# Moving five weight subtractions of GpSimd from the last attention heads to the rear of an expert

## The chip, the cores and the metric

One core of a Trainium2 chip runs the whole program in one launch. The metric is the device time of that launch in microseconds. The engines are named as in the profile: PE is TensorE, DVE is VectorE, ACT is ScalarE, POOL is GpSimd and SP is SyncE, which here issues only DMAs.

## What is computed

Input `x` has 1250 rows of 512 numbers; there are 20000 edges. Two blocks follow each other, each added to its input:

```
x = x + gnn(layernorm(x), edges)      # mean over neighbours, two matmuls, batch norm, relu
x = x + moe(layernorm(x))             # 4 experts, every row goes to its best 2

expert(xf, mask):
    h    = ln(xf);   q, k, v = split(h @ in_proj.T + b)          # 8 heads of 64
    a    = softmax(where(mask, q @ k.T / 8, -1e9));  o = (a @ v) @ out_proj.T + b
    x1   = xf + o
    return x1 + gelu(ln(x1) @ w1.T + b1) @ w2.T + b2              # hidden width 256
```

The change lies in the second block. All weights are used there as a sum of two f16 numbers: a high half, and a low half that is the f32 weight minus the high half.

## The kernel before, in words

The four experts run one after the other. A router gives each expert a list of rows; the program holds several bodies ("arms") for different list lengths and every engine branches to the same one. In this run the experts with numbers 0, 1 and 3 take a short arm of 4 row tiles (512 rows), and expert 2 takes the long arm of 10 row tiles (1280 rows). Here they are called the first, second, third and fourth expert.

The weights of an expert are ten pieces of 128 x 1024 numbers: six for the projections to q, k and v (`QKV_P`), two for the output projection, one for each of the two MLP matrices. A piece comes by DMA into one of five slots of `w_stage` (`load_piece`, L482), ACT writes the high half (`high_weights`, L856), and POOL writes the low half as the f32 piece minus the high half (`low_weights`, L587, one TENSOR_TENSOR at L590) and counts `s_elo`. Piece p + 5 may be loaded once the low half of piece p stands (L490), so the next expert's piece 5 waits for its piece 0, and its pieces 6 to 9 wait for its pieces 1 to 4. PE waits for the six projection pieces at L1639, in front of the first value product of the expert.

An expert has two parts. In the first, the heads, PE makes projections, scores and weighted sums, ACT the exponentials, DVE maxima of the scores and, for each pair of heads, the division by the sum of the exponentials (`divide_of`, L2258: a reciprocal L2265, a product L2266, and the two halves of the result L2267 and L2268; it needs ACT's copy of the sums, L1100). With ACT's last heads (`short_head`, L1109, heads 5 to 7; in the long arm spread over the last two heads) come the high halves of the next expert's six projection pieces, and POOL's six low halves stand in its own order behind its work for the heads.

In the second part, the rear, the work runs over pairs of row tiles. PE first runs 18 or 32 matmuls that nobody reads (L1702), then the output projection (`project_out`, L1704). DVE adds the rows (L2365) and takes their statistics (L2369 to L2377); POOL raises the variances to the power -1/2 (L829), one instruction for a pair of tiles; DVE normalises (`second_rows`, L2385); PE transposes (L1724); ACT applies the affine map (L968); DVE splits it into f16 halves (`split_columns`, L2109 and L2110); PE multiplies (L1423), ACT applies gelu (L1188), DVE splits again (L2398, L2399) and adds the expert's share to the running total (`part`, L2391; `give`, L2405). POOL fetches the running totals with indirect DMAs at the start of the rear (L817) and sends the finished rows away at its end (L835), each when `s_y` says that its tile is done.

All five engines run their own instruction lists in the written order; semaphores join them. POOL's list around the change is: the heads' copies, the six low halves of the next expert, the wait for the end of DVE's divisions (L811), the fetches with the powers between them, and the outgoing rows.

Of the kernel before, what the change touches and what calls it, by code (L numbers as in the profile page):

```python
# [29 lines left out]
NE = 4  # L30
# [18 lines left out]
QKV_P, OUT_P, W1_P = (W_OUT - W_QKV) // WP, W_1 // WP, W_2 // WP  # L49
# [111 lines left out]
def program(nc, x, src, dst, gnn_w, gnn_par, gate_w, gate_b, ew, epar_d, erow, out):  # L161
    stack = ExitStack()
    with stack:
# [422 lines left out]
        def _(pool):  # L586
            def low_weights(e, p):  # L587
                cols = slice(p * WP, (p + 1) * WP)
                pool.wait_ge(s_ehi, e * NWP + (p + 1))
                nc.gpsimd.tensor_tensor(w16[:, 1, cols], w_stage[:, p % WB, :], w16[:, 0, cols],  # L590
                                        ALU.subtract).then_inc(s_elo, 1)
# [128 lines left out]
            def expert_pool(e, shape):  # L720
# [14 lines left out]
                def copy_values(j, hd):  # L735
                    nc.gpsimd.tensor_copy(v_head[:, hd, 0:nt, hd * HD:(hd + 1) * HD],  # L736
                                          v_rows[:, 0:nt, bass.ds(j * P + hd * HD, HD)]).then_inc(s_vh, 1)

                def after_head():

                    summed.skip(nx)
                    pool.wait_ge(s_pv, summed.at(0))
                    pool.sem_inc(s_idle, 1)

                def values_of(j, hd):

                    t0 = j % 2 * nt
                    nc.gpsimd.tensor_copy(v_head[:, hd, t0:t0 + nt, hd * HD:(hd + 1) * HD],
                                          v_rows[:, 0:nt, j * P + hd * HD:j * P + (hd + 1) * HD]).then_inc(s_vh, 1)

                def second_head(j):

                    pool.wait_ge(s_split, splits.at(2 * j + 2))
                    pool.sem_inc(s_idle, 1)
                    if j in (0, 3):
                        pool.wait_ge(s_vh, e * H + (2, 0, 0, 8)[j])
                    else:
                        pool.wait_ge(s_elo, e * NWP + QKV_P + (0, 1, 3, 0)[j])
                    pool.sem_inc(s_idle, 1)
                    cols = slice(j % 2 * SHORT, j % 2 * SHORT + nt * P)  # L760
                    nc.gpsimd.tensor_copy(q_both[0:HD, 1, cols], halves[HD:P, 0, 0, cols])
                    nc.gpsimd.tensor_copy(k_both[0:HD, 1, cols], halves[HD:P, 1, 1, cols])
                    nc.gpsimd.tensor_copy(q_both[HD:P, 1, cols], halves[HD:P, 0, 1, cols])
                    nc.gpsimd.tensor_copy(k_both[HD:P, 1, cols], halves[HD:P, 1, 0, cols]).then_inc(s_qkc, 1)
                    pool.wait_ge(s_qkc, seconds.at(j + 1))
                    pool.sem_inc(s_idle, 1)

                if shape.short:
                    values_of(0, 0)
                    values_of(0, 1)  # L770
                    pool.wait_ge(s_scat, 16 * 2 * NT)
                    second_head(0)
                    values_of(1, 0)
                    values_of(1, 1)
                    low_weights(e, QKV_P)
                    second_head(1)
                    for j in (2, 3):
                        for hd in range(2):
                            pool.wait_ge(s_pv, summed.at((2 * j - 4 + hd + 1) * nx))
                            pool.sem_inc(s_idle, 1)  # L780
                            values_of(j, hd)
                            if QKV_P + 2 * j - 3 + hd < NWP:
                                low_weights(e, QKV_P + 2 * j - 3 + hd)
                        second_head(j)
                    summed.skip(8 * nx)
                    splits.skip(8)
                    seconds.skip(H // 2)
                    with nc.gpsimd.If(e < NE - 1):
                        for p in range(QKV_P):
                            low_weights(e + 1, p)  # L790
                else:
                    for hd in range(2):
                        nc.gpsimd.tensor_copy(v_head[:, hd, 0:nt, hd * HD:(hd + 1) * HD], v_rows[:, 0:nt, hd * HD:(hd + 1) * HD]
                                              ).then_inc(s_vh, 1)
                    for p in range(QKV_P, NWP):
                        low_weights(e, p)
                    summed.settle()
                    with nc.gpsimd.Fori(0, H // 2 - 1) as j:
                        after_head()
                        copy_values(j + 1, 0)  # L800
                        after_head()
                        copy_values(j + 1, 1)
                        summed.settle()
                    summed.skip(2 * nx)
                    splits.skip(8 * len(shape.spans))
                    with nc.gpsimd.If(e < NE - 1):
                        for p in range(QKV_P):
                            low_weights(e + 1, p)


                pool.wait_ge(s_attended, e + 1)  # L811
# [11 lines left out]
                for p in range(shape.np):  # L823
# [4 lines left out]
                    pool.sem_inc(s_idle, 1)  # L828
                    nc.gpsimd.tensor_tensor(l2r[:, mine], l2mv[:, mine, 1], l2half[:, mine], ALU.pow).then_inc(s_l2r, 1)  # L829
                stats.skip(shape.np)  # L830
                for t in range(nt):

                    pool.wait_ge(s_y, added.at(t + 1))
                    pool.sem_inc(s_idle, 1)
                    nc.gpsimd.indirect_dma_start(  # L835
                        out=out, out_offset=bass.IndirectOffsetOnAxis(ap=token[:, t:t + 1], axis=0),
                        in_=total_rows[:, t, :], in_offset=None, bounds_check=N - 1,
                        oob_is_err=False).then_inc(s_back_out if t < UP else s_back_up, 16)
# [11 lines left out]
            for e, shape in chosen(nc, nc.gpsimd, "pool", arms):  # L850
                expert_pool(e, shape)
# [1644 lines left out]
```

## Time and profile before

| | us |
|---|---|
| three timed runs | 1276.58, 1280.37, 1280.38 (median 1280.37) |
| the profiled execution | 1276.06 |
| its span, first to last instruction | 1274.1 |
| PE busy | 1045.5 (82%) |
| DVE busy | 735.9 (58%) |
| ACT busy | 454.5 (36%) |
| POOL busy | 319.6 (25%) |
| the low halves on POOL (L590), 35 of them | 75.6 |

The first table row is what the runs took; the others belong to one profiled execution, and every duration and moment below is of that one, in microseconds from the start of its span. A busy share is an average over the span and says nothing on what ends a stage; that is read from the chain of waits and from the order in time. The rear of the first expert lies at about 496 to 531, that of the second at 636 to 672, that of the third at 1044 to 1114 and that of the fourth at the end.

### The profile page before, as it was taken

The page shows a single profiled execution, that of the slowest core. Times are in us where ns is not written, and L with a number is a line of the kernel's source. Part 1 is how long each engine was busy: PE and PEld are TensorE (multiplying, and loading weights), DVE is VectorE, ACT ScalarE, POOL GpSimd, SP SyncE. Part 2 cuts the span into 40 slices and gives each one's busy share as a digit, 9 for nine tenths or more (in the row PEclk, how much of TensorE's full clock was granted, in tenths as well). Part 3 has the DMA queues.
Part 4 walks back from the last instruction along what each step waited for, and adds up shares of the span by engine and source line. Part 5 has one row for each costly group of instructions (what it writes and reads, how often), then busy time and mean ns, then how long its engine had stood idle before and what let it go on. Part 6 is the DMA issues. An engine that isn't in the chain of part 4 may idle for free.

```text
span 1274.1 us, 19526 instructions
## 1 busy us (share of the span) xinstructions
PE 1045.5 (82%) x5148; PEld 565.6 (44%) x5149; DVE 735.9 (58%) x1609; ACT 454.5 (36%) x847; POOL 319.6 (25%) x300
## 2 busy tenths in 40 slices
PE   1986789999936878688786989899897999889984
PEld 1654467778523433334343434344343335433333
DVE  5385534352383578537864674756748248646753
ACT  1301112222423553436625334434344532236521
POOL 3102233443538435114420030000000133313211
PEclk9987789999967989899897989999999999989997
DMA  5194000000358315201503020000002121110010
GB/s 154 46 247 122 1 2 0 0 0 1 124 150 233 103 34 196 71 11 50 182 24 124 1 67 1 1 0 0 0 0 100 34 63 49 74 41 1 2 32 35
DMA packets 36366, 75.64 MB, mean 59 GB/s; under 512 B 9739, under 2 KB 10037, under 8 KB 36010
## 3 DMA queue, kind: packets, MB, share of 16 engines
q1 hardware_dynamic: 27658, 55.91, 14.6%
q0 software_dynamic: 8320, 16.49, 4.5%
q10 hardware_dynamic: 288, 2.10, 0.4%
q8 instruction: 40, 0.66, 0.2%
q14 instruction: 60, 0.49, 0.1%
HBM read 49.06 MB, written 26.70 MB: 59 GB/s over the span
## 4 chain that ended last, share of the span: by engine, by line
PE 63%; DVE 16%; issue 9%; ACT 4%; POOL 3%; DMA 1%; DVEq 1%; SPq 0%; ACTq 0%; POOLq 0%
PE bank L1423 16%; PE bank L1514 9%; PE bank L1271 8%; PE bank L1310 5%; PE bank L1544 3%; PE bank L1599 3%; DVE den L2265 3%; PE bank L1478 2%; PE bank L1306 2%; PE bank L1499 2%; PE bank L1501 2%; PE bank L1238 2%; POOL lists L688 2%; DVE oT L2267 1%; PE bank L1558 1%
## 5 line engine op out<-in xcount | busy, mean ns | idle before, releaser
L1876 DVE TENSOR_SCALAR oh_src<-iota,edge 125x1250 f16 x178 | 101.4, 570 | 106.2 <-PE bank L1271 101.3
L1514 PE MATMUL bank<-probs_t,v_head 128*128 128x512 f32 (+1 forms) x288 | 147.0, 594 | 6.8 <-ACT probs_t L1056 6.2
L1056 ACT ACTIVATE probs_t<-bank 128x512 f32<-128x512 f32 x144 | 81.5, 573 | 136.0 <-PE bank L1501 135.4
L2178 DVE TENSOR_REDUCE mx<-bank 128x1 f32<-128x512 f32 x144 | 88.5, 656 | 63.9 <-PE bank L1478 63.0
L1271 PE MATMUL bank<-oh_src,oh_dst 125*125 x534 | 111.3, 359 | 2.8 <-issue 0.6
L590 POOL TENSOR_TENSOR w<-w_stage,w 128x1024 f16<-128x1024 f32 x35 | 75.6, 2172 | 139.5 <-ACT w L858 139.5
L1599 PE MATMUL bank<-probs_t,v_head 128*128 128x128 f32 (+2 forms) x192 | 88.3, 547 | 6.9 <-ACT probs_t L1107 5.1
L1423 PE MATMUL bank<-hT,w 128*128 128x256 f16 (+1 forms) x552 | 88.9, 325 | 1.4 <-DVE hT L2110 1.4
L1271 PEld LDWEIGHTS bank<-oh_src,oh_dst 125*125 x534 | 70.6, 142 | 43.7 <-issue 24.6
L1544 PE MATMUL bank<-hT,w 128*128 128x512 f16 x288 | 73.3, 388 | 10.1 <-ACT t L1081 9.8
L1423 PE MATMUL bank<-w,hT 128*128 128x512 f16 x264 | 65.8, 402 | 8.5 <-DVE hT L2110 8.5
L1107 ACT ACTIVATE probs_t<-bank 128x128 f32<-128x128 f32 (+2 forms) x96 | 44.6, 487 | 75.7 <-PE bank L1585 70.2
L2251 DVE TENSOR_REDUCE mx<-bank 128x1 f32<-128x128 f32 (+2 forms) x96 | 48.9, 551 | 39.3 <-PE bank L1558 38.9
L1423 PEld LDWEIGHTS bank<-hT,w 128*128 128x128 f16 (+1 forms) x552 | 56.7, 103 | 32.8 <-issue 2.8
L1514 PEld LDWEIGHTS bank<-probs_t,v_head 128*128 128x128 f32 x288 | 53.1, 195 | 29.3 <-ACT probs_t L1056 14.5
L1423 PE MATMUL bank<-w,oT 128*128 128x512 f16 x264 | 64.2, 396 | 0.0
L968 ACT ACTIVATE t<-bank,ep 128x256 f32<-128x256 f32 x44 | 21.2, 562 | 110.2 <-PE bank L1724 110.2
L736 POOL COPY v_head<-x_in 128x640 f32 x6 | 4.3, 722 | 223.3 <-PE bank L1514 223.3
L1478 PE MATMUL bank<-k_hi,q_hi 66*128 66x512 f16 x144 | 44.0, 382 | 18.8 <-DVE mx L2178 10.8
L1499 PE MATMUL bank<-q_hi,k_hi 97*128 97x512 f16 x144 | 54.9, 381 | 2.8 <-ACT q_hi L1034 2.7
L879 ACT COPY a_row<-bank 125x512 f32<-125x512 f32 (+1 forms) x30 | 13.3, 515 | 118.4 <-PE bank L1284 118.4
L1501 PE MATMUL bank<-q_both,k_both 128*128 128x512 f16 x144 | 54.4, 378 | 0.0
(323 smaller groups left out, 1934.8 us busy)
## 6 DMA issues: line engine op xcount, KB each, us to landing
w_stage<-in_ew_dram SPq DMA_DIRECT2D x40, 512.0 KB, 4.2
lists<-zeros SPq DMA_DIRECT2D x1, 10340.0 KB
x_in<-lists SPq DMA_DIRECT2D x15, 517.0 KB, 5.8
x_mem<-lists SPq DMA_DIRECT2D x3, 1024.0 KB, 5.2
x_mem<-lists SPq DMA_DIRECT2D x1, 2560.0 KB, 10.4
out_dram<-x_mem SPq DMA_DIRECT2D x10, 250.0 KB
table<-rows SPq DMA_DIRECT2D x5, 449.8 KB
big<-in_x_dram SPq DMA_DIRECT2D x10, 224.0 KB
```

What stands on the lines that cost most here:

```text
L590: nc.gpsimd.tensor_tensor(w16[:, 1, cols], w_stage[:, p % WB, :], w16[:, 0, cols], ALU.subtract).then_inc(s_elo, 1)
L1056: nc.scalar.activation(probs_t[:, x % NPB, 0:cn], stb[x % 2][:, 0:cn], ACT.Exp).then_inc(s_exp, 1)
L1271: last = nc.tensor.matmul(ab[k][0:TT, 0:cn], oh_dst[:, bass.ds(slot, 1), i, :], oh_src[:, bass.ds(slot, 1), i, c0:c0 + cn], start=False, s ...
L1423: last = nc.tensor.matmul(bank, lhs(a, c), rhs(b, c), start=(n == 0 and c == 0 and bias is None), stop=(n == 2 and c == chunks - 1))
L1478: nc.tensor.matmul(sbk[i % 2][:, 0:cn], q_hi[0:MARK + 2, hd, t * P:(t + 1) * P], k_hi[0:MARK + 2, hd, c0:c0 + cn], start=True, stop=True). ...
L1499: nc.tensor.matmul(stb[i % 2][:, 0:cn], k_hi[0:SHIFT + 1, hd, kt * P:(kt + 1) * P], q_hi[0:SHIFT + 1, hd, c0:c0 + cn], start=True, stop=False)
L1501: nc.tensor.matmul(stb[i % 2][:, 0:cn], k_both[:, hd, kt * P:(kt + 1) * P], q_both[:, hd, c0:c0 + cn], start=False, stop=True).then_inc(s_ ...
L1514: nc.tensor.matmul(pvb[(hd * nq + s) % 2][:, 0:cn], v_head[:, hd, kt, :], probs_t[:, (hd * nx + i) % NPB, 0:cn], start=(k == 0), stop=(k = ...
L1544: last = nc.tensor.matmul(pp[0][:, 0:nt * P], w16[:, a, c0:c0 + P], hT[b][:, c, 0:nt * P], start=k == 0, stop=k == 3 * KC - 1)
L1599: nc.tensor.matmul(pvb[(hd * nq + s) % 2][:, 0:cn], v_head[:, hd, j % 2 * nt + kt, :], probs_t[:, i, 0:cn], start=(k == 0), stop=(k == nk ...
L1876: nc.vector.tensor_scalar(oh_src[:, bass.ds(slot, 1), i, 0:N].rearrange("p a n -> p (a n)"), iota[:, :], edge[:, 0, i, bass.ds(g, 1)], Non ...
L2178: nc.vector.tensor_reduce(mx[:, hd, t, s:s + 1], sbk[i % 2][:, 0:cn], AX.X, ALU.max).then_inc(s_mx, 1)
```

## The change

Of the six low halves for the next expert, piece 0 stays where it was, behind POOL's work for the heads. The other five are issued later in POOL's list: behind the last power of the row statistics, and ahead of the waits for finished rows. Both arms are changed alike. The same 35 subtractions are run, on the same data, under the same condition (not in the last expert).

```diff
@@ expert_pool, short arm (the long arm has the same edit)
                     with nc.gpsimd.If(e < NE - 1):
-                        for p in range(QKV_P):
-                            low_weights(e + 1, p)
+                        low_weights(e + 1, 0)
@@ expert_pool, rear
                     nc.gpsimd.tensor_tensor(l2r[:, mine], l2mv[:, mine, 1], l2half[:, mine], ALU.pow).then_inc(s_l2r, 1)
                 stats.skip(shape.np)
+                with nc.gpsimd.If(e < NE - 1):
+                    for p in range(1, QKV_P):
+                        low_weights(e + 1, p)
                 for t in range(nt):
 
                     pool.wait_ge(s_y, added.at(t + 1))
```

## Rows read from the trace of the kernel before

**Rows 1.** The page, part 4: share of the span on the chain that ended last.

```profile
PE 63%; DVE 16%; issue 9%; ACT 4%; POOL 3%; DMA 1%; DVEq 1%; SPq 0%; ACTq 0%; POOLq 0%
```

**Rows 2.** Timeline of POOL, first expert: start, duration, engine, line, operation [idle before <-releaser].

```profile
491.08 4.26 POOL L590 TENSOR_TENSOR w<-w_stage,w 128x1024 f16<-128x1024 f32 x2 [1.76 <-ACT w L858]
...
511.62 0.74 POOL L829 TENSOR_TENSOR l2r<-l2mv,l2half 128x2 f32<-128x2 f32 x1 [4.82 <-DVE l2mv L2377]
527.41 1.05 POOL L835 DMA_INDIRECT out_dram<-total_rows,token  x1 [15.05 <-DVE total_rows L2405]
```

**Rows 3.** Timeline of DVE, first expert, last two divisions of the heads.

```profile
482.55 0.29 DVE L2266 TENSOR_TENSOR o_pair<-o_pair,den 128x128 f32<-128x128 f32 x1
...
486.05 1.29 DVE L2266 TENSOR_TENSOR o_pair<-o_pair,den 128x384 f32<-128x384 f32 x1
487.38 2.17 DVE L2267 TENSOR_SCALAR oT<-o_pair,ep 128x384 f16<-128x384 f32 x1
...
491.09 2.27 DVE L2266 TENSOR_TENSOR o_pair<-o_pair,den 128x128 f32<-128x128 f32 x1
493.40 2.03 DVE L2267 TENSOR_SCALAR oT<-o_pair,ep 128x128 f16<-128x128 f32 x1
...
495.73 2.54 DVE L2265 RECIPROCAL den<-den 128x384 f32<-128x384 f32 x1
498.31 0.56 DVE L2266 TENSOR_TENSOR o_pair<-o_pair,den 128x384 f32<-128x384 f32 x1
498.90 0.42 DVE L2267 TENSOR_SCALAR oT<-o_pair,ep 128x384 f16<-128x384 f32 x1
```

**Rows 4.** Timeline of ACT, same stretch: its copies of the sums.

```profile
489.68 0.26 ACT L1100 COPY den<-bank 64x128 f32<-64x128 f32 x1
...
492.46 0.47 ACT L1100 COPY den<-bank 64x384 f32<-64x384 f32 x1
```

**Rows 5.** Timeline of PE, from the heads into the rear.

```profile
491.13 4.16 PE L1702 MATMUL bank<-hT,ident_h 128*128 128x512 f16 x18
496.04 0.38 PE L1420 MATMUL bank<-bias_rows,ones_k 33*128 33x512 f16 x1 [0.74 <-DVE oT L2268]
...
500.03 0.39 PE L1420 MATMUL bank<-bias_rows,ones_k 33*128 33x512 f16 x1 [0.92 <-DVE oT L2268]
```

**Rows 6.** Timeline of POOL, third expert: four low halves back to back.

```profile
736.70 8.36 POOL L590 TENSOR_TENSOR w<-w_stage,w 128x1024 f16<-128x1024 f32 x4
```

**Rows 7.** Timeline of DVE beside them: the first and the last of four.

```profile
736.69 2.15 DVE L2122 TENSOR_SCALAR share<-place,first_n 128x10 f32<-128x10 f32 x1
...
743.04 2.37 DVE L2168 COPY q_hi<-halves 64x1280 f16<-64x1280 f16 x1
```

**Rows 8.** Timeline of POOL, fourth expert: one low half.

```profile
1176.88 2.47 POOL L590 TENSOR_TENSOR w<-w_stage,w 128x1024 f16<-128x1024 f32 x1 [6.73 <-ACT w L858]
```

**Rows 9.** Timeline of DVE beside it.

```profile
1177.28 2.61 DVE L2223 TENSOR_TENSOR halves<-t,halves 128x512 f16<-128x512 f32 x1
```

**Rows 10.** Timeline of DVE, first expert's rear, behind the last power.

```profile
512.90 0.69 DVE L2110 TENSOR_TENSOR hT<-t,hT 128x512 f16<-128x512 f32 x1
513.51 1.00 DVE L2385 TENSOR_SCALAR probs_t<-x_mem,l2mv,l2r 128x512 f32<-128x512 f32 x2
```

**Rows 11.** Timeline of PE, what it waits for there.

```profile
514.64 1.43 PE L1724 MATMUL bank<-ident,probs_t 128*128 128x128 f32 x8 [4.62 <-DVE probs_t L2385]
```

**Rows 12.** Timeline of POOL, third expert's rear: the last power.

```profile
1089.30 0.73 POOL L829 TENSOR_TENSOR l2r<-l2mv,l2half 128x2 f32<-128x2 f32 x1 [12.21 <-DVE l2mv L2377]
```

**Rows 13.** Timeline of DVE, third expert's rear.

```profile
1090.58 0.69 DVE L2110 TENSOR_TENSOR hT<-t,hT 128x512 f16<-128x512 f32 x1
...
1093.08 0.69 DVE L2399 TENSOR_TENSOR k_both<-probs_t,q_both 128x512 f16<-128x512 f32 x1
```

**Rows 14.** Timeline of PE, third expert's rear.

```profile
1096.13 1.09 PE L1724 MATMUL bank<-ident,probs_t 128*128 128x128 f32 x8 [2.13 <-DVE probs_t L2385]
```

**Rows 15.** Stretch: length, busy and count of PE, PEld, DVE, ACT, POOL; PE clock, DMA share, GB/s.

```profile
514.60:520.00 5.40, 5.36 (x34) 4.30 (x35) 3.47 (x6) 1.93 (x4) 0.00 (x0) 0.68 0.01 3
```

More of the change, by code:

```diff
@@ L806, in expert_pool @@
                     with nc.gpsimd.If(e < NE - 1):
-                        for p in range(QKV_P):
-                            low_weights(e + 1, p)
+                        low_weights(e + 1, 0)
                 pool.wait_ge(s_attended, e + 1)
```

## The prediction

> **What bounds the kernel now.** I read the chain that ended last, then the timelines around each place where POOL's subtractions lie now and will lie. The chain [rows 1] belongs to PE for 63% and to DVE for 16%; POOL holds 3%. So neither the 2.13 us that a subtraction takes (4.26 for two [rows 2]) nor its place in POOL's list matters by itself. What matters is whom a subtraction holds up.
>
> That is to be seen in the last heads. DVE's product L2266 on 384 columns takes 0.56 us when POOL is idle and 1.29 us beside POOL's pair of subtractions; L2267 takes 0.42 us and then 2.17; on 128 columns L2266 takes 0.29 us and then 2.27 [rows 3]. The stalled instruction of DVE ends just behind the end of a subtraction, and the reciprocal between them keeps its time. The cleanest place is the third expert, where four subtractions run back to back in 8.36 us [rows 6]: in that time DVE gets four instructions done, one for each subtraction, three of them on 10 columns, and each over 2 us long (the first and the last of the four in [rows 7]). DVE and POOL take turns, instruction by instruction, and a turn of POOL's costs DVE 2.1 us. With a 512-column instruction of DVE between, the turn is longer: a subtraction took 2.47 us and ended at 1179.35, and DVE's product of the kind that splits columns ended 0.54 us behind it [rows 8, 9]. I use 2.45 us for a turn with full-width instructions on both sides; the bounds are 2.09 (8.36 / 4) and 2.61.
>
> **What leaves the heads.** In the first expert DVE loses there 0.73 + 1.75 + 1.98 + 1.74 = 6.2 us, against the free durations [rows 3] (for L2267 on 128 columns I take that of L2266). The first two sit in front of a division that cannot start before ACT's copy of the sums ends at 489.94 [rows 4], and it started there (its product follows at 491.09 [rows 3]): they are hidden already. Without the other two, DVE reaches the last division at about 492, and ACT's copy for it ends at 492.93 [rows 4]. So it starts there and not at 495.73: 2.8 us. It runs for 4.30 us to the release of PE at 500.03 [rows 3, 5], which would be 497.2. But PE has its own reason to be late: 18 unread matmuls until 495.29 [rows 5], then the first output projection, which takes 4.0 us with its wait and 3.0 without, and only then the second, at about 498.35. The saving that reaches the chain is 500.03 - 498.35 = 1.7 us. The second expert has the same order of the same instructions, with one stall shifted from L2266 to L2268, and gives 1.7 us too. In the third expert the divisions of the last heads are hardly touched by the subtractions (they lie apart, one at a time) and I take 0. The fourth has none. Sum: **-3.4 us**. Bounds: 0, if PE is late by something else, and -12.4 (6.2 twice), if all of the blocked time came back.
>
> **What arrives in the rear.** The five subtractions are ready at once there: their high halves have long stood. They start when the last power ends, at 512.36 in the first expert [rows 2]; with the branch, about 512.7. From there five turns last to about 524.6. POOL's next duty is at 527.41 [rows 2], so the outgoing rows are not late. DVE is another matter, for from the last power on it is dense and the chain hangs on it: a product L2110 at 512.90, two normalisations L2385 until 514.51 [rows 10], for which PE has already waited 4.62 us [rows 11]. By the turns, L2110 waits for the first subtraction (to 515.3), the first L2385 for the second (subtraction ends 517.25), the second L2385 for the third (ends 519.65) and is done at 519.95. That is 5.4 us late. What follows on DVE meets subtractions four and five while PE transposes and multiplies for some 5 us, and is done at about 526, as PE gets there: 0. The rear of the second expert has the same instructions in the same order. Bounds for each: 2.1 (one turn on the chain) and 10.7 (all five). I take **+5.4 twice**, as the count of three turns follows from the written order.
>
> In the third expert the last power ends at 1090.03 [rows 12], the first subtraction starts at about 1090.3, and DVE has no gap at all: L2110 at 1090.58, then two L2391, L2398 and L2399 until 1093.77 (first and last of five in [rows 13]) and then, behind two more, the L2385 for which PE waits at 1096.13 [rows 14]. Each of these five takes a turn: the fifth subtraction ends at 1090.3 + 2.2 + 4 x 2.45 = 1102.3, L2399 at 1102.8 and not 1093.77. That is 9.1 us late, with bounds 7.3 (turns of 2.09) and 10.3 (2.61 and the full own time). PE has work until 1094.0 and then nothing before L2385, and what follows its wait is 17 us of dense matmuls, so nothing is caught up: **+9.1 us**.
>
> PE's pause there grows from 2.1 to 11 us. Behind the pause of 4.62 us in the first expert eight transposes took 1.43 us [rows 11] and the granted clock was 0.68 over the next 5.4 us [rows 15]: part of it at the 1.2 GHz level, the rest at 2.4. Behind 2.13 us they took 1.09 [rows 14]. The stretch of 5.4 us at 0.68 costs 5.4 x (1 - 0.68) = 1.7 us: **+1.7 us**, bounds 0 and 3. In the first two experts the pause is paid already.
>
> The DMAs: pieces 6 to 9 of the next expert now wait for subtractions in the rear and are issued there, some 30 us later. Nobody needs them before the next expert's heads, 40 us on: 0. The wait of PE for the six projection pieces (L1639) lies behind the end of the rear; the last subtraction ends 7 us before the last outgoing row in the first expert, and in the third about 1102.3 against 1114: 0. There the ten outgoing rows start later than before, but they are 1.3 us apart and the last one waits for the last tile anyway: 0.
>
> **A rule on this.** The Trainium skill, "SBUF — State Buffer", section "Who interferes with whom", says that GpSimd's port is DVE's second pair, and that DVE instructions with two SBUF inputs, or casts, copies and tensor_scalar in a 2-port mode, exclude a GpSimd instruction and are excluded by it, while one SBUF input outside those modes is free. The trace agrees: L2266, L2267 and the copy are stalled, the reciprocal is not. By the page the normalisation and the cast of the rear, which never meet a subtraction in this trace, are stalled as well, and the sum is that below; if only the forms with two inputs were, it would be that of the second rival. The page adds that issue order decides who blocks, which speaks for the first rival below.
>
> **Sum.** -3.4 + 10.8 + 9.1 + 1.7 = +18.2 us. The profiled execution takes 1276.06 with its span of 1274.1 in it, so the changed kernel would take 1294.3 in such an execution. The three timed runs lie at 1276.6 once and at 1280.4 twice; I add to the middle of the two, 1278.4, and predict **1297 us**.
>
> **The rivals.**
> 1. *POOL is the one that waits in the rear.* DVE is dense there, its instructions start first, and POOL's subtractions squeeze into gaps (15 us of idle POOL in the first expert). Then the rear costs nothing and the heads return between 3.4 and 12.4 us: 1266 to 1275 from the same base; in the likelier part, -3.4, it is within the noise. It decides if a subtraction started in a dense stretch lasts much longer than 2.5 us. Against it: in both places where the trace has pairs or more, DVE got exactly one instruction per subtraction, dense or not [rows 6, 7]. Chance 0.12: 0.05 faster, 0.07 no change.
> 2. *Normalisation and cast are not stalled*, only the forms with two inputs. L2385 writes f32 and no row shows it beside POOL; but L2267, the same operation with f16 out, is stalled. Then the first two rears cost 2 us each, the third still four turns, 7.5, and the clock: -3.4 + 4 + 7.5 + 1.7 = +9.8, or 1288 us. Chance 0.10.
> 3. *All five turns on the chain in each rear.* The splitting of columns behind PE's transposes meets subtractions four and five, and if it lies on the chain, each of the first two rears costs up to 10.7: +18.2 + 10.6 = +29, or 1307 us. For it: PE's second product waits for it, and by my count is only just in time. Chance 0.08.
>
> My forecast has 0.70. About 3.8 us (0.3%) is what a measurement of this kernel can tell from none. Faster 0.05, same 0.07, slower 0.88. The range 1286 to 1307 holds the forecast with its bounds and rivals 2 and 3, and leaves rival 1 out.
>
> **What would show it.** In the profile after: L2266 to L2268 of the last heads at 0.3 to 0.6 us, and the second output projection of the first expert about 1.7 us earlier. In the rear, five subtractions in a row, 11.5 to 12.5 us long, and beside them L2110 and L2385 at about 2.4 us each. PE's wait for L2385 (L1724) near 10 us in the first two experts and 11 in the third. The forecast is wrong if L2385 keeps 0.5 us beside a subtraction, if the subtractions are stretched in DVE's place, or if the first rear loses far from 5.4 us or the third far from 9.

## The result, and the profile after

The changed kernel takes 1299.34 us (median of 4 runs, 1297.37 to 1301.09) against 1278.47 for the kernel before, whose runs in the same comparison lie between 1274.87 and 1280.38. The ratio is 1.0152, with a 95% interval of 1.0127 to 1.0176: 1.5% slower, or 19.4 us with 16.2 to 22.5. The forecast was 1297 us.

The lines behind line 787 of the changed kernel have other numbers: on POOL the fetches are L815 (before: L817), the power is L827 (before: L829), the outgoing rows L836, and on DVE, ACT and PE each number is one higher (the normalisation is L2386, the split L2110 and L2111). The chain that ended last is hardly another one by engine; page, part 4, of the kernel after:

```profile
PE 64%; DVE 14%; issue 9%; ACT 5%; POOL 3%; DMA 1%; DVEq 1%; SPq 1%; ACTq 0%; POOLq 0%
```

So shares do not tell where 20 us went. The timelines do. First the heads of the first expert, DVE of the kernel after (columns as in [rows 2]); these lines answer to [rows 3]:

```profile
492.55 0.95 DVE L2266 RECIPROCAL den<-den 128x128 f32<-128x128 f32 x1 [2.06 <-ACT den L1101]
493.54 0.29 DVE L2267 TENSOR_TENSOR o_pair<-o_pair,den 128x128 f32<-128x128 f32 x1
493.87 0.29 DVE L2268 TENSOR_SCALAR oT<-o_pair,ep 128x128 f16<-128x128 f32 x1
...
495.55 2.55 DVE L2266 RECIPROCAL den<-den 128x384 f32<-128x384 f32 x1 [1.01 <-ACT den L1101]
```

The stalls are gone, 2.27 and 2.03 us have become 0.29 each, and both divisions now wait for ACT. PE of the kernel after, answering to [rows 5]:

```profile
493.72 4.36 PE L1703 MATMUL bank<-hT,ident_h 128*128 128x512 f16 x18
498.01 0.39 PE L1421 MATMUL bank<-bias_rows,ones_k 33*128 33x512 f16 x1
...
501.02 0.39 PE L1421 MATMUL bank<-bias_rows,ones_k 33*128 33x512 f16 x1
```

The pauses in front of both output projections, 0.74 and 0.92 us in [rows 5], are no longer there: PE's own unread matmuls end the wait. Then the rear. POOL of the kernel after, first expert and third, answering to [rows 2, 12]:

```profile
512.60 0.74 POOL L827 TENSOR_TENSOR l2r<-l2mv,l2half 128x2 f32<-128x2 f32 x1 [5.53 <-DVE l2mv L2378]
513.33 11.48 POOL L590 TENSOR_TENSOR w<-w_stage,w 128x1024 f16<-128x1024 f32 x5
...
1102.44 0.74 POOL L827 TENSOR_TENSOR l2r<-l2mv,l2half 128x2 f32<-128x2 f32 x1 [12.20 <-DVE l2mv L2378]
1103.14 12.03 POOL L590 TENSOR_TENSOR w<-w_stage,w 128x1024 f16<-128x1024 f32 x5
```

The five subtractions take 11.48 and 12.03 us: 2.3 and 2.4 us each, a little over the 2.13 us of one alone. Beside them DVE, first expert, answering to [rows 10]:

```profile
513.44 2.34 DVE L2110 CAST hT<-t 128x512 f16<-128x512 f32 x1
515.81 2.49 DVE L2111 TENSOR_TENSOR hT<-t,hT 128x512 f16<-128x512 f32 x1
518.23 4.60 DVE L2386 TENSOR_SCALAR probs_t<-x_mem,l2mv,l2r 128x512 f32<-128x512 f32 x2
525.23 0.43 DVE L2110 CAST hT<-t 128x512 f16<-128x512 f32 x1 [2.41 <-ACT t L969]
```

and third expert, answering to [rows 13]:

```profile
1103.27 2.35 DVE L2110 CAST hT<-t 128x512 f16<-128x512 f32 x1
1105.65 2.50 DVE L2111 TENSOR_TENSOR hT<-t,hT 128x512 f16<-128x512 f32 x1
1108.07 5.13 DVE L2392 SCALAR_TENSOR_TENSOR total_rows<-x_mem,share,total_rows 128x512 f32<-128x512 f32 x2
1113.12 2.34 DVE L2399 CAST q_both<-probs_t 128x512 f16<-128x512 f32 x1
1115.49 0.69 DVE L2400 TENSOR_TENSOR k_both<-probs_t,q_both 128x512 f16<-128x512 f32 x1
```

DVE gets one instruction done per subtraction, and each takes 2.3 to 2.6 us. These are casts (L2110, L2399), a product (L2111), normalisations (L2386) and `part` (L2392). The first instruction after the fifth subtraction has its 0.43 or 0.69 us again. PE, first and third expert, answering to [rows 11, 14]:

```profile
522.96 1.96 PE L1725 MATMUL bank<-ident,probs_t 128*128 128x128 f32 x8 [11.94 <-DVE probs_t L2386]
...
1118.58 1.97 PE L1725 MATMUL bank<-ident,probs_t 128*128 128x128 f32 x8 [11.44 <-DVE probs_t L2386]
```

PE waits 11.9 us where it waited 4.6, and 11.4 where it waited 2.1. And it comes back slower; stretches of the kernel after (columns of [rows 15]), the 5.4 us behind each of these two waits:

```profile
522.90:528.30 5.40, 5.34 (x25) 4.27 (x26) 3.00 (x6) 1.93 (x4) 1.91 (x1) 0.50 0.45 140
1118.50:1123.90 5.40, 5.32 (x32) 4.49 (x32) 2.97 (x6) 1.93 (x4) 1.43 (x2) 0.64 0.33 126
```

The granted clock is 0.50 over the whole first stretch, all of it at the 1.2 GHz level, against 0.68 before [rows 15].

**The stages.** A single execution starts its first expert up to 9 us earlier or later than another. So I measure stages between two marks of the same trace: in a short expert, from POOL's copies for the last pair of heads (L761, at 470.49 before) to the start of the last `give` (L2405, at 530.56). The third rear is measured from the first output projection (its first L1423) to the last `give`, and "between" is from the last `give` of the second expert to that projection. In us:

| kernel | timed ratio to before [95%] | first | second | between | third rear |
|---|---|---|---|---|---|
| before | 1 | 60.07 | 59.14 | 373.28 | 68.74 |
| after | 1.0152 [1.0127, 1.0176] | 66.56 | 65.44 | 370.44 | 79.88 |
| loads_late | 0.9988 [0.9960, 1.0016] | 60.07 | 59.15 | 373.18 | 68.79 |
| none_in_rear | 0.9945 [0.9921, 0.9969] | 59.48 | 58.40 | 370.72 | 68.77 |
| short_only | 1.0086 [1.0056, 1.0115] | 66.49 | 65.42 | 370.43 | 68.74 |
| long_only | 1.0064 [1.0035, 1.0092] | 59.87 | 59.11 | 373.27 | 79.88 |
| two_in_rear | 1.0066 [1.0035, 1.0097] | 63.01 | 61.92 | 370.54 | 75.31 |
| fill_in_rear | 1.0039 [1.0018, 1.0060] | 62.91 | 62.13 | 373.69 | 69.85 |
| early_rear | 0.9983 [0.9963, 1.0003] | 59.13 | 58.32 | 370.66 | 68.74 |
| early_14 | 0.9994 [0.9968, 1.0019] | 57.34 | 57.27 | 375.75 | 70.40 |
| before_warm | 0.9960 [0.9929, 0.9991] | 58.20 | 58.55 | 374.06 | 70.34 |
| early_warm | 0.9939 [0.9920, 0.9957] | 56.64 | 55.68 | 373.25 | 68.74 |

The change adds 6.49 + 6.30 + 11.14 and takes 2.84 off between: 21.1 us, inside the measured interval of 16.2 to 22.5. The ratios come from 4 to 12 runs of a kernel, but each row of stages from one trace.

### The profile page after: what moved, and what is told of

Its sections match the earlier page's. It is cut to its first block, busy times and chain, and to the rows that moved or that the text cites. A ratio compares the mean times of both kernels' runs of the same rounds, so it can differ in the third digit from the quotient of the medians.

```text
span 1298.5 us, 19530 instructions
## 1 busy us (share of the span) xinstructions
PE 1051.4 (81%) x5148; PEld 570.7 (44%) x5149; DVE 748.2 (58%) x1609; ACT 454.5 (35%) x847; POOL 322.5 (25%) x300
## 4 chain that ended last, share of the span: by engine, by line
PE 64%; DVE 14%; issue 9%; ACT 5%; POOL 3%; DMA 1%; DVEq 1%; SPq 1%; ACTq 0%; POOLq 0%
PE bank L1424 16%; PE bank L1515 9%; PE bank L1272 8%; PE bank L1311 5%; PE bank L1600 3%; PE bank L1545 3%; PE bank L1307 2%; PE bank L1479 2%; PE bank L1500 2%; PE bank L1502 2%; PE bank L1239 2%; DVE den L2266 2%; POOL lists L688 2%; PE bank L1559 1%; PE bank L1294 1%
## 5 line engine op out<-in xcount | busy, mean ns | idle before, releaser
L590 POOL TENSOR_TENSOR w<-w_stage,w 128x1024 f16<-128x1024 f32 x35 | 78.3, 2253 | 87.8 <-ACT w L859 87.8
L1545 PE MATMUL bank<-hT,w 128*128 128x512 f16 x288 | 73.5, 389 | 11.4 <-ACT t L1082 11.4
L1515 PEld LDWEIGHTS bank<-probs_t,v_head 128*128 128x128 f32 x288 | 53.0, 195 | 29.2 <-ACT probs_t L1057 14.7
L815 POOL DMA_INDIRECT total_rows<-out_dram,token x22 | 23.1, 1052 | 127.0 <-DVEq L2359 121.7
## 6 DMA issues: line engine op xcount, KB each, us to landing
x_mem<-lists SPq DMA_DIRECT2D x1, 2560.0 KB, 10.2
```

The lines of the kernel that those rows point to most:

```text
L1515: nc.tensor.matmul(pvb[(hd * nq + s) % 2][:, 0:cn], v_head[:, hd, kt, :], probs_t[:, (hd * nx + i) % NPB, 0:cn], start=(k == 0), stop=(k = ...
L1545: last = nc.tensor.matmul(pp[0][:, 0:nt * P], w16[:, a, c0:c0 + P], hT[b][:, c, 0:nt * P], start=k == 0, stop=k == 3 * KC - 1)
```

## The experiments

**1. Is it the transfers?** Moving the subtractions also moves the release of the next expert's pieces 6 to 9. `loads_late` moves the release alone (`s_gmean` is a semaphore that nothing else uses any more by then):

```diff
 # heads, both arms
-                            low_weights(e + 1, p)
+                            low_weights(e + 1, p, s_gmean if p else None)   # counts s_gmean, not s_elo
 # rear, behind the last power
+                with nc.gpsimd.If(e < NE - 1):
+                    pool.wait_ge(s_gmean, e * (QKV_P - 1) + QKV_P)   # s_gmean starts at 1
+                    pool.sem_inc(s_elo, QKV_P - 1)
```

> Kernel before, but the count that releases the DMAs of the next expert's pieces 6 to 9 is raised for pieces 1 to 5 only in the rear, at the place where the changed kernel has the five subtractions; the subtractions themselves stay in the heads. Theory (POOL and DVE take turns at a port, so a subtraction stops DVE): no change against before, within 2 us, and in the first expert's rear PE's wait for L2385 stays near 4.6 us. Rival (the late transfers, or PE waiting for the released pieces, cost the time): most of the 19 us slower appears here too.

Measured: 0.9988 [0.9960, 1.0016], and no stage moves by more than 0.1 us. PE of this kernel in the first rear:

```profile
519.91 1.40 PE L1727 MATMUL bank<-ident,probs_t 128*128 128x128 f32 x8 [4.62 <-DVE probs_t L2388]
```

The wait is 4.62 us as before. The late transfers cost nothing.

**2. Is it the subtractions?** `none_in_rear` leaves the five subtractions of the rear out and raises their semaphore at the same place, so the low halves of these pieces are those of another expert.

```diff
 # changed kernel, rear
-                    for p in range(1, QKV_P):
-                        low_weights(e + 1, p)
+                    pool.wait_ge(s_ehi, e * NWP + (NWP + QKV_P))
+                    pool.sem_inc(s_elo, QKV_P - 1)
```

> Changed kernel with the five subtractions of the rear left out (the low halves of these pieces are then those of another expert); their semaphore is raised at the same place, so the transfers go as in the changed kernel. Theory: the rear is as in the kernel before and the heads are relieved, so 3.4 us faster than before, 22 us faster than the changed kernel; PE waits 4.6 us for L2385 in the first rear and 2.1 us in the third. Rival (late transfers): still some 15 us slower than before.

Measured: 0.9945 [0.9921, 0.9969] of before, which is 7.0 us faster (4.0 to 10.1); expected were 3.4. The third rear is back at 68.77 and the waits of PE are 4.62 and 2.17 us. So the rear's whole loss is the subtractions and what follows from them. But the first and second experts gain only 0.6 and 0.7 us and not 1.7 each, while 2.6 us come from the stretch between. In both places PE's clock differs. PE of this kernel, and the stretch behind its wait:

```profile
515.37 1.97 PE L1725 MATMUL bank<-ident,probs_t 128*128 128x128 f32 x8 [4.62 <-DVE probs_t L2386]
```

```profile
515.30:520.70 5.40, 5.33 (x25) 4.29 (x26) 2.98 (x6) 1.93 (x4) 0.00 (x0) 0.50 0.81 322
```

The pause is as long as in [rows 11], but now all of the 5.4 us behind it are at 0.50 and not at 0.68: the heads' relief (the second output projection starts 27.76 us behind the mark, against 29.54 in the kernel before: 1.8 us earlier) gives 1.2 us back here. Between, the kernels with that relief can gain. In the kernel before, in the first head of the third expert, PE waits for DVE's copies and is slow behind that wait, on the chain. In the changed kernel the slow stretch falls earlier, beside the wait. Before, and then after, 10 us each, the first of each pair starting 64 to 65 us behind the end of the second expert:

```profile
735.00:745.00 10.00, 7.37 (x30) 3.04 (x30) 9.87 (x11) 5.65 (x11) 9.68 (x6) 1.00 0.40 113
745.00:755.00 10.00, 7.33 (x15) 3.09 (x16) 5.53 (x12) 1.20 (x3) 0.06 (x1) 0.66 0.27 97
```

```profile
751.50:761.50 10.00, 8.22 (x24) 3.20 (x25) 9.87 (x11) 4.47 (x9) 9.71 (x6) 0.66 0.41 112
761.50:771.50 10.00, 9.54 (x35) 4.12 (x33) 7.83 (x16) 3.44 (x7) 0.03 (x1) 1.00 0.30 98
```

What decides in which of the two the clock falls was not tested. The values of "between" are 370.4 to 370.7 in five kernels and 373.2 and more in the other seven. All five have the relieved heads of the short arm, but so have `fill_in_rear`, `early_14` and `early_warm` of the seven. So the relief alone does not decide it, and a kernel can win or lose 2.8 us there for no merit of its own.

**3. One arm at a time.** `short_only` has the change in the short arm alone, `long_only` in the long arm alone:

```diff
+                if shape.short:            # long_only: if not shape.short; the arm left as before keeps its six in the heads
                     with nc.gpsimd.If(e < NE - 1):
                         for p in range(1, QKV_P):
                             low_weights(e + 1, p)
```

> Only the short arm (first and second expert) is changed, the long one is as before. Theory: from the trace of the changed kernel 6.5 + 6.3 = 12.8 us slower than before (1.0%). By the sizes of the prediction (three turns on the chain instead of four) it would be 7.4 us. Rival (all of it in the long arm, where POOL's outgoing rows start late): no change.

> Only the long arm (third expert) is changed. Theory: 9.3 us of turns and 1.8 us of PE's clock, 11.1 us slower than before (0.9%). Rival (the outgoing rows, which here start late, hold up the fourth expert): more than 11 us, with the fourth expert starting more than 11 us late against the end of the rear's last matmul.

Measured: 1.0086 [1.0056, 1.0115], 11.0 us, and 1.0064 [1.0035, 1.0092], 8.2 us. The stages are those of the full change where the arm is changed (66.49 and 65.42; 79.88) and those of before where it isn't, so the parts add up. The 12.8 us expected of `short_only` left out the stretch between: with its -2.85 the stages give 9.9 us, and both lie in the interval of 7.2 to 14.7. The timed 8.2 us stand against 11.1 by stages, inside the interval of 4.5 to 11.8. The fourth expert does not start later than the third rear ends, so POOL's outgoing rows cost nothing: from the last `give` of the third expert to POOL's last second-head copies (L761) in the fourth are 85.54 us in `long_only`, against 86.03 before.

**4. By the number.** Four subtractions in the heads, two in the rear:

```diff
-                        low_weights(e + 1, 0)          # heads, both arms
+                        for p in range(0, 4):
+                            low_weights(e + 1, p)
-                    for p in range(1, QKV_P):          # rear
+                    for p in range(4, QKV_P):
```

> Four subtractions in the heads as before, two (pieces 4 and 5) in the rear behind the last power. Theory (each subtraction in the rear costs DVE one turn, 2.4 us less the 0.5 us or so that the instruction takes anyway): two turns, about 3.8 us in each of three rears, PE's wait for L2385 about 4.6 + 3.9 in the first; heads relieved by 1.7 us twice as in the full change; PE's clock in the third 1 to 1.8 us: +9 to +10 us, about half of the full change. Rival (a fixed cost of having any subtraction there, or of the late transfers): the same +19 us as the full change.

Measured: 1.0066 [1.0035, 1.0097], 8.5 us (4.5 to 12.4), less than half of the full change's 19.4, where 9 to 10 were expected. DVE of this kernel, first rear:

```profile
515.10 2.35 DVE L2112 CAST hT<-t 128x512 f16<-128x512 f32 x1
517.48 2.49 DVE L2113 TENSOR_TENSOR hT<-t,hT 128x512 f16<-128x512 f32 x1
519.89 0.99 DVE L2388 TENSOR_SCALAR probs_t<-x_mem,l2mv,l2r 128x512 f32<-128x512 f32 x2
```

Two instructions are stopped, and the two normalisations behind them are free, at 0.5 us each. PE's waits:

```profile
521.02 1.97 PE L1727 MATMUL bank<-ident,probs_t 128*128 128x128 f32 x8 [8.34 <-DVE probs_t L2388]
...
1107.58 1.96 PE L1727 MATMUL bank<-ident,probs_t 128*128 128x128 f32 x8 [5.78 <-DVE probs_t L2388]
```

They are 3.72 and 3.65 us longer than before: 1.8 us a turn. In the third rear the rest of its +6.57 us is clock, for the slow stretch lasts longer than in the full change: 2.9 us for a pause of 5.8, against 1.8 for one of 11.4.

**5. Reading or being there.** The subtractions of the rear become memsets of the low halves, which write but read nothing:

```diff
-                        low_weights(e + 1, p)
+                        cols = slice(p * WP, (p + 1) * WP)
+                        pool.wait_ge(s_ehi, e * NWP + (NWP + p + 1))
+                        pool.sem_inc(s_idle, 1)
+                        nc.gpsimd.memset(w16[:, 1, cols], 0.0).then_inc(s_elo, 1)
```

> Changed kernel, but each of the five subtractions of the rear is replaced by a memset of the same 128 x 1024 f16 numbers (the low halves of these pieces are then zero). A memset of this size took 0.97 us elsewhere in the kernel; it writes and reads nothing. Theory with the rule of the Trainium skill, page SBUF - State Buffer, section Who interferes with whom: DVE's two-input products (L2111, L2392) are not stopped, casts and normalisations (L2110, L2386) are, up to 1 us each. From rows: five turns of at most 1.0 us, 0 to 3 us in each rear, -3.4 in the heads: between -3 and +5 us against before. If only reading is exclusive: nothing is stopped and it equals the kernel without the subtractions.

Measured: 1.0039 [1.0018, 1.0060], 5.0 us slower than before (2.3 to 7.7), at the upper end of what was expected. POOL and DVE of this kernel in the third rear:

```profile
1101.11 5.07 POOL L834 MEMSET w<- 128x1024 f16 x5
```

```profile
1101.25 1.09 DVE L2113 CAST hT<-t 128x512 f16<-128x512 f32 x1
1102.37 0.69 DVE L2114 TENSOR_TENSOR hT<-t,hT 128x512 f16<-128x512 f32 x1
1102.98 1.41 DVE L2395 SCALAR_TENSOR_TENSOR total_rows<-x_mem,share,total_rows 128x512 f32<-128x512 f32 x2
1104.31 0.98 DVE L2402 CAST q_both<-probs_t 128x512 f16<-128x512 f32 x1
```

The two casts are stopped for one memset each; the products with two inputs in SBUF keep their 0.69 and 0.70 us beside the memsets, which beside the subtractions took 2.5. This is the division that the Trainium skill makes in "SBUF — State Buffer", "Who interferes with whom": two SBUF inputs contend only with a GpSimd instruction that reads, a 2-port mode with any. The forms with one input were tested on casts alone: no normalisation met a memset. What nothing led me to expect is the first rear:

```profile
515.54 4.51 POOL L834 MEMSET w<- 128x1024 f16 x5
```

```profile
515.67 4.66 DVE L2113 CAST hT<-t 128x512 f16<-128x512 f32 x1
520.36 0.69 DVE L2114 TENSOR_TENSOR hT<-t,hT 128x512 f16<-128x512 f32 x1
```

There one cast waits for all five memsets, and in the second rear it takes 4.66 us again. That DVE gets a turn after each instruction of POOL's holds for the subtractions in every trace, but not for these memsets. Why the third rear differs from the first two stays open.

**6. A place without turns.** In the short arm, pieces 4 and 5 are subtracted right behind the end of the divisions, where DVE only adds out of PSUM and takes statistics, and the fetches are put behind the first power:

```diff
 # kernel before, heads of the short arm
-                        for p in range(QKV_P):
+                        for p in range(4):
                             low_weights(e + 1, p)
 # rear
-                fetch(0)
+                if shape.short:
+                    with nc.gpsimd.If(e < NE - 1):
+                        for p in range(4, QKV_P):
+                            low_weights(e + 1, p)
+                else:
+                    fetch(0)
                 for p in range(shape.np):
 ...
+                    if shape.short and p == 1:
+                        fetch(0)
+                        fetch(1)
-                    if p + 1 < shape.np:
+                    if not shape.short and p + 1 < shape.np:
```

> Kernel before, but in the short arm pieces 4 and 5 are subtracted at the very start of the rear, right behind the end of DVE's divisions and ahead of the first power, and the four fetches come behind the first power instead of ahead of it. DVE has there only additions with one input in PSUM and statistics with one input, of kinds that no row shows stopped, until the first small operation of L2377. Theory: the relief of the heads (1.7 us in each of two experts, 3.4 in all) without a turn on the chain: 3 us faster than before (0.2 to 0.3%). Rival (the additions with one PSUM input are stopped too, or the late fetches hold up the shares): 4 us or more slower than that, so no gain or a loss.

Measured: 0.9983 [0.9963, 1.0003]: 2.2 us faster (-0.4 to 4.7), not told from before. But DVE is not stopped in this place. POOL and DVE of this kernel:

```profile
499.65 4.21 POOL L590 TENSOR_TENSOR w<-w_stage,w 128x1024 f16<-128x1024 f32 x2 [8.91 <-DVEq L2366]
```

```profile
499.84 0.69 DVE L2373 TENSOR_TENSOR x_mem<-bank,x_mem 128x512 f32<-128x512 f32 x1 [0.17 <-PE bank L1431]
500.57 0.69 DVE L2377 BATCH_NORM_STATS2 l2st<-x_mem 128x6 f32<-128x512 f32 x1
502.77 0.69 DVE L2373 TENSOR_TENSOR x_mem<-bank,x_mem 128x512 f32<-128x512 f32 x1 [1.50 <-PE bank L1431]
```

Beside two subtractions an addition with one input in PSUM and the statistics keep 0.69 us. The relief of the heads arrives (1.8 us in each), and about half of it goes to the clock as in experiment 2: 0.94 and 0.82 us are left.

**7. The clock.** 18 unread matmuls in PE's pause, ahead of the transposes that wait for the normalisation, in the kernel before and in `early_rear`; and `early_rear` with 14 instead of 18 unread matmuls at the end of the heads:

```diff
                 for step in range(np + 3):
 ...
+                    if shape.short and step == 2:
+                        for k in range(18):
+                            nc.tensor.matmul(pvb[k % 2][:, :], ident_h[:, :], w16[:, 0, W_OUT:W_OUT + D],
+                                             start=True, stop=True)
                     if 1 <= step <= np:
                         turn_second(step - 1)
```

> Kernel before with 18 unread matmuls put into PE's pause ahead of the transposes that wait for L2385 in the short arm (before their wait). Theory of the clock (the pause lets the granted clock fall, and the 5.4 us behind it run at 0.5 to 0.68 of full speed): the clock stays near 1.00 there, the eight transposes take 1.0 us instead of 1.4 to 1.9 and the 48 products 5.4 instead of 6.4 to 6.8: 1.4 to 1.8 us in each of three short experts, 4 to 5 us faster than before. Rival (the clock does not depend on what PE does in the pause): no change.

> early_rear with the same 18 unread matmuls in PE's pause. Theory: the relief of the heads (1.8 us in each of the first two experts, of which 1.0 was lost to a clock of 0.50 behind the pause) and the clock kept: 2.5 us in the first two short experts beside the 0.9 of early_rear, 1.5 in the last, 8 us or more faster than before (0.6%). Rival: as early_rear.

> The kernel early_rear with 14 instead of 18 unread matmuls between the heads and the rear in the short arm. Theory: with the turns gone from the heads, PE's own unread matmuls are what the first output projection waits for (0.23 us each), so four fewer start it 0.9 us earlier in each of three short experts, up to 2.5 us less than early_rear, unless the last division (about 1.1 us ahead of the second projection) or a lower clock takes it back. Rival (the projection still waits for DVE's divisions): no change against early_rear.

Measured: before_warm 0.9960 [0.9929, 0.9991], early_warm 0.9939 [0.9920, 0.9957], early_14 0.9994 [0.9968, 1.0019]. PE of early_warm, first rear, and the stretch behind the wait:

```profile
512.05 4.05 PE L1768 MATMUL bank<-w,ident_h 128*128 128x512 f16 x18
516.84 1.09 PE L1732 MATMUL bank<-ident,probs_t 128*128 128x128 f32 x8 [0.73 <-DVE probs_t L2397]
517.76 2.78 PE L1431 MATMUL bank<-hT,w 128*128 128x256 f16 x24
```

```profile
516.80:522.20 5.40, 4.98 (x44) 4.32 (x45) 3.47 (x6) 3.48 (x6) 0.00 (x0) 1.00 0.01 3
```

The clock stays at 1.00, and the first expert takes 56.64 us against 59.13 without them: 2.5 us, as expected. early_warm is the fastest kernel here, 7.8 us (5.5 to 10.2) below before and some 27 below the change.

before_warm is 5.1 us (1.2 to 9.1) below before, where 4 to 5 were expected. From PE's transposes to the last `give` it takes 14.26 us in each short expert, against 15.92, 15.93 and 16.82. Yet its second expert as a whole gains only 0.6 us. There the clock in the first 6 us behind the mark is 0.50 and not 0.72, and the second output projection starts 1.1 us later.

early_14 shows that PE's matmuls bound the relief in the first expert: the second output projection starts 0.94 us earlier than in early_rear. In the second expert it does not (26.83 us behind the mark against 26.81), for there too the clock in the first 6 us behind the mark is lower, 0.53 against 0.72. The first two stages are 1.8 and 1.1 us shorter than those of early_rear, and 0.9 and 1.1 of this lie behind PE's pause, where the clock lost less. It loses 5.1 us between and 1.7 in the third rear, in an arm that it does not touch, so its whole time shows no gain. The third rear is the clock: behind the same pause of 2.13 us the granted clock over the next 5.4 us is 1.00 in the kernel before and in early_rear, 0.68 in early_14 and 0.70 in before_warm, which loses 1.6 us there. The 5.1 us between were not taken apart.

## Why the prediction was right

**The heads, -1.7 us twice: right.** The second output projection starts 27.69 us behind the mark against 29.54: 1.85 us earlier, and 1.82 in the second expert (26.81 against 28.63). The first pair of stalls was hidden behind ACT, as worked out, and the unread matmuls were the next bound (early_14, first expert).

**The rear of the short arm, +5.4 us twice: right in kind, too small.** From the end of the last power to the end of the normalisation took 2.15 us before and takes 9.49: 7.3 us more. The step that failed is "with the branch, about 512.7". The branch costs POOL no time that shows: the first subtraction starts as the power ends, at 513.33. So it also catches the cast in front of the product, and four turns lie on the chain instead of three. The size of a turn (2.45 us) and the rule of one instruction each were right, and splitting behind PE's transposes met no subtraction (0.43 us at 525.23), so rival 3 fell. It fell narrowly: the fifth subtraction had ended 0.4 us before.

**"In the first two experts the pause is paid already": wrong.** From the start of the transposes to the last `give` took 15.92 us and takes 16.93; in the second expert 15.93 and 16.72. The clock had not been at its low level all the way before. That is 1.8 us in all. The longer pause is not needed for it: in `none_in_rear` the pause is the old one, 4.62 us, and these stretches take 17.12 and 17.00.

**The third rear, +9.1 and +1.7 us: right.** From the end of the power to PE's transposes 6.10 us became 15.40, 9.3 more, and from there to the last `give` 16.78 became 18.62, 1.8 more. The count of five turns was safe from the error of the first rear: the cast in front of the first product is stopped here too, but with five subtractions there are no more than five turns, and the last product (L2400) went free.

**Costs put at nothing: right.** Transfers (experiment 1) and the outgoing rows (experiment 3).

**Not foreseen: -2.8 us** in the first head of the third expert, where PE's slow stretch lies off the chain in the kernel after. Why it lies there is not shown (experiment 2). It happens to cancel half of the 3.8 + 1.8 us that the short rears cost beyond the forecast. So it is luck that +18.2 us came as near to the measured 19.4 as it did.

Rival 1 fell with POOL's 11.48 us for five (2.3 each: POOL is held only for DVE's instruction, DVE for POOL's). Rival 2 fell with L2386 at 2.3 us a piece.

## What to carry to other kernels

A GpSimd instruction that is off every chain can still cost its full length, if DVE has an instruction with two SBUF inputs, a cast or a tensor_scalar at that time: price its place by what DVE has to do beside it, not by GpSimd's idle time. The free places here were DVE's reciprocals (2.55 us for 384 columns with or without a subtraction beside them), its reductions (1.02 us for two), its additions out of PSUM and its statistics (0.69 us each). And when a wait is removed or made longer, look at the granted clock behind the next pause of PE; unread matmuls in a pause of 4.6 us gave back 1.7 to 2.7 us behind it each time here, though one expert lost 1.1 of them again in its heads.

## What the runs showed of the hardware beyond that

In the rears DVE gets exactly one instruction in per GpSimd subtraction, and loses 1.8 us a turn. Against five memsets in a row a cast got in after the first one in one rear (1.09 us) and only after the last in the two others (4.66 us each). The slow stretch behind a pause of PE of the same 4.62 us had a mean clock of 0.68 in one kernel and 0.50 in another, a difference of 1.2 us in the first expert, with nothing changed behind the pause. Behind the same pause of 2.13 us in the third rear it was 1.00 in the kernel before and 0.70 in before_warm, which differs from it in the other arm alone: 1.6 us.
